# Three-piece hand-over of the first layer's one-hot tables, unread matmul streams in the second layer, zero-padded attribute matmul in the fourth

## The reference, cut to what matters

```python
h = jnp.maximum(_layernorm(x, axis=-1), 0.0)
x = x + _L0_gnn_ref(h, edge_attr_32, L0_gnn_eps, src, dst)      # relu(h[src] + edge_attr), summed over dst
h = jnp.maximum(_layernorm(x, axis=-1), 0.0)
x = x + _L1_gnn_ref(h, src, dst, edge_attr_3, edge_attr_10, edge_weight, L1_gnn_W1, L1_gnn_W2)
...
x = x + _L2_gnn_ref(h, src, dst)                                # degree-normalized sum
...
x = x + _L3_gnn_ref(h, src, dst, edge_attr_4, edge_attr_8, L3_gnn_fc_w1, L3_gnn_fc_w2)
```

```python
h = 2.0 ** 0.5 * jax.nn.relu(emb @ W1 / 10.0 ** 0.5)
w = (h @ W2 / 16.0 ** 0.5).reshape(E, 7, MUL, MOUT)
...
s_act = TANH_GAIN * jnp.tanh(s_out)
gates = TANH_GAIN * jnp.tanh(g_out)
edge_ftr = jnp.concatenate([s_act, (gates[:, :, None] * v_out).reshape(E, 24)], axis=1) * norm[:, None]
return jax.ops.segment_sum(edge_ftr, edge_dst, num_segments=N)
```

## Time and profile before

| | |
|---|---|
| timed runs | 23265.71, 23264.34, 23223.69 us, median 23264.34 |
| the profiled execution | 23142.48 us (span 23140.8) |
| busy share of the span | PE 64%, PEld 47%, DVE 54%, ACT 32%, POOL 43% |
| granted TensorE clock, mean | 0.715 of full speed |
| layer 0, about 395 to 6394 us | clock 0.60 in the middle, DMA share 0.63 |
| layer 1, about 6500 to 16130 us | clock 0.70 |
| layer 3, about 17190 to 23070 us | clock 0.83 |

### The profile page before, as it was taken

One profiled execution on the slowest core, in us unless ns is written; L12 is line 12 of the kernel. 1 busy time (PEld: TensorE's weight loads), 2 busy tenths in 40 slices (PEclk: granted clock), 3 DMA queues, 4 the chain that ended last, 5 costly groups with the idle time before them and its releaser, 6 DMA issues. The chain is left out here.

```text
span 23140.8 us, 410176 instructions
## 1 busy us (share of the span) xinstructions
PE 14747.1 (64%) x107469; PEld 10941.2 (47%) x108092; DVE 12537.1 (54%) x29165; ACT 7316.3 (32%) x22555; POOL 10030.6 (43%) x11407
## 2 busy tenths in 40 slices
PE   2444443433357777777777777777667777777777
PEld 1333333333345555555555555555445555555555
DVE  5455444554445555555555555555026666666666
ACT  1333333333323333333333333333002222222222
POOL 4455444454434444444444444443014555555554
PEclk7565655566667776777767777776888888888887
DMA  4666666666611111111111111110851111111111
GB/s 89 80 87 88 83 82 81 84 84 82 79 29 20 20 20 20 20 20 20 20 20 20 20 20 20 20 20 16 341 222 17 17 17 17 17 17 17 17 17 17
DMA packets 3048984, 1153.55 MB, mean 50 GB/s; under 512 B 2631873, under 2 KB 2993198, under 8 KB 3047249
## 3 DMA queue, kind: packets, MB, share of 16 engines
q1 hardware_dynamic: 2236554, 930.37, 19.8%
q0 software_dynamic: 312320, 178.52, 5.7%
q10 hardware_dynamic: 500000, 43.28, 2.3%
HBM read 767.02 MB, written 383.38 MB: 50 GB/s over the span
## 5 line engine op out<-in xcount | busy, mean ns | idle before, releaser
L1349 POOL DMA_INDIRECT w_rows<-table,w_idx x9375 | 8966.0, 956 | 6981.3 <-issue 2969.3
L1574 PE MATMUL w_p_w<-w_w,w_ht 128*128 128x256 f32 x12500 | 3743.4, 454 | 746.8 <-DVE w_prodv L1516 378.7
L1331 PE MATMUL w_p_deg<-w_hot_lo,w_hot_row 128*128 128x196 bf16 x6250 | 1956.2, 355 | 2574.5 <-issue 1210.7
L1574 PEld LDWEIGHTS w_p_w<-w_w,w_ht 128*128 128x128 f32 x12500 | 2762.7, 229 | 1717.7 <-issue 639.4
L1925 PE MATMUL w_p_xe<-w_xt,w_pick_b 128*128 128x128 bf16 x12500 | 1691.8, 279 | 1998.9 <-ACT w_xt L1911 1810.3
L1787 DVE TENSOR_TENSOR w_prod<-w_p_xe,w_he 128x512 f32<-128x512 f32 x3125 | 2123.7, 688 | 1012.7 <-PE w_p_xe L1925 999.1
L1734 POOL TENSOR_TENSOR w_dots<-w_v,w_unit 128x240 f32<-128x240 f32 x625 | 400.1, 640 | 4518.6 <-issue 3491.5
L1925 PEld LDWEIGHTS w_p_xe<-w_xt,w_pick_b 128*128 128x128 bf16 x12500 | 1032.9, 122 | 2762.5 <-ACT w_xt L1911 1665.2
L1145 ACT ACTIVATE w_dist<-row_iota,w_negrel 128x32 f32<-128x32 f32 x9375 | 2178.8, 313 | 442.6 <-issue 262.8
L1305 ACT CAST w_counts<-w_p_count 128x784 bf16<-128x784 f32 x1875 | 1237.1, 705 | 3410.6 <-remote 2107.1
L1331 PEld LDWEIGHTS w_p_deg<-w_hot_lo,w_hot_row 128*128 128x128 bf16 x6250 | 878.3, 141 | 2756.8 <-issue 1855.5
(11 more groups left out here) (209 smaller groups left out, 21512.5 us busy)
## 6 DMA issues: line engine op xcount, KB each, us to landing
counts<-w_counts SPq DMA_DIRECT2D x1250, 245.0 KB
d_rows<-counts SPq DMA_DIRECT2D x388, 784.0 KB
w_rows<-table,w_idx POOLq DMA_INDIRECT x9375
w_rel_row<-rel_row SPq DMA_DIRECT2D x625, 120.0 KB
w_edge<-e SPq DMA_DIRECT2D x625, 80.0 KB
w_idx<-src SPq DMA_DIRECT2D x1875, 2.5 KB
w_negrel<-negrel SPq DMA_DIRECT2D x1875, 2.5 KB
w_nodes<-split SPq DMA_DIRECT2D x1875, 2.0 KB
```

Source lines behind the costliest of these rows:

```text
L1331: nc.tensor.matmul(p_deg[:], hot_row[s2][:, b, :], hot_lo[s2][:, b, :], start=False, stop=False, skip_group_check=True)
L1349: pool.indirect_dma_start(out=rows[:, t, :], out_offset=None, in_=table[0:N, :], in_offset=bass.IndirectOffsetOnAxis(ap=idx[:, t:t + 1], a ...
L1574: last = nc.tensor.matmul(p_w[:, t * 256:(t + 1) * 256], ht[g.slot(2)][:, k, t * P:(t + 1) * P], w2[:, k, :], start=k == 0, stop=k == 1)
```

## The change

Three edits, one for each of the loops:

```diff
@@ window_pass_0, DVE
-                    vec.tensor_tensor(hot_row[s2][:], spread(p_iota[:, 0:P], [P, PAIRS_G, P], 1),
-                                      spread(pair[s][:, :, 0], [P, PAIRS_G, P], 2), ALU.is_equal)
+                    for b0, b1 in PIECES:
+                        bs, n = slice(2 * b0, 2 * b1), 2 * (b1 - b0)
+                        vec.tensor_tensor(hot_row[s2][:, bs, :], spread(p_iota[:, 0:P], [P, n, P], 1),
+                                          spread(pair[s][:, bs, 0], [P, n, P], 2), ALU.is_equal)
+                        vec.tensor_tensor(hot_lo[s2][:, bs, :], spread(p_iota[:, P:], [P, n, SRC_LO], 1),
+                                          spread(pair[s][:, bs, 1], [P, n, SRC_LO], 2), ALU.is_equal).then_inc(pair_hot_ready, 1)
                     done(dve, emb_high, g)
                     free(dve, emb_low, g, 1)
                     vec.tensor_sub(emb_rest[:], emb[s][:], emb_parts[s][:, 0, :]).then_inc(emb_left, 1)
-                    vec.tensor_tensor(hot_lo[s2][:], spread(p_iota[:, P:], [P, PAIRS_G, SRC_LO], 1),
-                                      spread(pair[s][:, :, 1], [P, PAIRS_G, SRC_LO], 2), ALU.is_equal).then_inc(pair_hot_ready, 1)
@@ window_pass_0, PE
-                    done(pe, pair_hot_ready, g)
                     for i, (b0, b1) in enumerate(PIECES):
+                        pe.wait_ge(pair_hot_ready, g.times(len(PIECES), i + 1))
                         wait_count(pe, count_moved, g.times(len(PIECES), i + 1 - len(PIECES)))
@@ window_pass_3: setup, then DVE, then PE
-        hidden = StackedEmbedding(nc, a, 3, sb, HID3)
+        hidden = StackedEmbedding(nc, a, 3, sb, HID3, P)
+        still = sb("still", [P, P + 256], BF16)
+            vec.memset(still[:], 0.0)
                         wait_count(pe, w_used, g.times(len(BANKS), bank + 1 - len(BANKS)))
+                        if t1 == T:
+                            for _ in range(4):
+                                nc.tensor.matmul(p_w[:, T * 256:], still[:, 0:P], still[:, P:], start=True, stop=True)
@@ window_pass_1, PE
+            def stream(times):
+
+                for _ in range(times):
+                    nc.tensor.matmul(p_he[:, 0:512], ident_b[:], pick_b[:].rearrange("p i e -> p (i e)"), start=True, stop=True)
+
                     wg.product(pe, g)
                     free(pe, he_ready, g, 1)
                     free(pe, xt_ready, g, 2)
+                    stream(6)
                     for c0, c1 in ((0, 512), (512, GE)):
```

## The result

The changed kernel takes 23972.81 us in the median of three runs (23908.48 to 24071.28), against 23264.34 before: a ratio of 1.0315 with a 95% interval of 1.0256 to 1.0374, +708 us. The forecast was 23812, slower, in 23050 to 24300.

The account below looks back on a forecast made before the run. It took a loop of waits, not a full engine, to bound layer 1. Terms of 745 - 200 + 0 gave +545 us on the profiled 23142; scaled to the timed median, 23812 us, range 23050 to 24300.

Parts of the forecast that it names:

- Layer 1, every round long: Layer 1: the streams make ACT's cast start behind POOL's gather burst in every group; 16.55 us a group, +745 us.
- The 0.3 us for the held expansion: Layer 1: the last expansion's signal may be held in the burst too; 0 to 0.6 us a group, taken as 0.3.
- a cast cannot be released inside the burst when its matmuls are not done in it: Layer 1: transposes delayed to around or past the burst's end make the cast late, costing 0.89 us a group.
- The clock: Layer 1: streams fill PE before the idle stretch, not in it, so `p_out` still takes 2.39 us.
- the first rival: Layer 1: streams keep the clock at full through `p_out`; 15.05 us a group, -195 us, whole kernel 22870; chance 13%.
- Layer 0, -200 us: Layer 0: PE starts earlier on pieces, saving two fifths of SP's wait; -200 us, in -480 to +150.
- Layer 3, 0 us: Layer 3: the four added matmuls hide in PE's idle time and zero rows add no columns; 0, between -100 and +200.
- PE's idle 2.07 us a group would take in the added work: Layer 3: PE's idle time hides four matmuls of 256 columns, +250 to +500 us if nothing hid them.
- The sum: Whole kernel: 745 - 200 + 0 = +545 us on the profiled execution of 23142 us, giving 23687.

Follow-up runs that it names:

- the first pair: The kernel before and the fully changed kernel as first measured: 23264.34 us and 23972.81 us, ratio 1.0315.
- `e5_all`: All three layers' edits together against the kernel before, on another chip with held signals: 23610.27 us against 22960.0, ratio 1.0292.
- the second run: Layer 1's six streams ahead of the transposes; alone, added to the kernel before: 23027.15 us against 22960.0, ratio 1.0041.
- The first run: Layer 1's six streams ahead of the hidden units; alone, added to the kernel before: 23721.85 us against 22960.0, ratio 1.0324.
- `e2_streams`: Only layer 1's twelve streams added to the kernel before, on a chip without held signals: 17390.86 us against 15797.12, ratio 1.1008.
- `e10_early_and_pieces`: Kernel before with layer 0's three pieces, layer 1's transposes ahead of the last expansion and ACT's cast ahead of its vector-weights copy: 22706.23 us, ratio 0.9801.
- `e13_narrow_stills_again`: Kernel before with only layer 3's four zero matmuls, 16 columns wide, no zero rows, signals held: 23349.3 us against 23158.21, ratio 1.008.

## Why the prediction was right in the time and wrong in two steps

- **Layer 1, every round long**: right. 45% of the rounds were long before and 100% after, at 16.51 us, with 16.55 forecast (+719 us against +745). The 0.3 us for the held expansion was +0.26 over 16.25 in the first pair, but `e5_all`, the same kernel, has just 16.25, so that term lies within the scatter.
- **Layer 1, what makes them long**: wrong. The step that failed is "a cast cannot be released inside the burst when its matmuls are not done in it", with the second run as its cause. It was never put to use: the transposes were to end at or past the burst's end, 3.7 us or more later, but with both runs they end 2.5 us later and still 1.4 us ahead of that end. Alone, the second run costs 0.4%; its transposes end 1.1 us later and the share of long rounds stays at 49%. The first run does it alone (+3.2%, 100% long), by carrying the last expansion and the vector weights deeper into the burst, ahead of the transposes' signal. I had priced that as a side effect of 0 to 0.6 us; it was the cause. That layer 1 came out within 26 us is therefore partly luck: with both runs in the kernel, either cause makes every round long, and a long round's length had been read from the trace of before.
- **The clock**: right for `p_out`. The mean in layer 1 rose from 0.70 to 0.78, but `p_out` took 2.40 us in the place where it took 2.39. By the groups by line (count, busy us, mean ns of one), here of the changed kernel from 7200 to 15400, then of `e2_streams`, where the clock was 1.00, a matmul of it took 420 ns and not 280:

```profile
L1981 PE MATMUL w_p_low<-w_stack,w_sgt 128*128 128x64 f32 x4969 | 1164.9, 420 | 13.3 <-ACT w_sgt L1868 7.3
```

```profile
L1974 PE MATMUL w_p_low<-w_stack,w_sgt 128*128 128x64 f32 x5390 | 715.4, 280 | 49.2 <-ACT w_sgt L1861 30.8
```

  The streams did move the clock, though. Counted from the trace's clock record, in the median group full clock came 0.3 us behind the burst's start and ended 0.7 us behind its end before; in the changed kernel it came 0.4 us ahead of the start and ended 2.5 us behind the end. `p_out` starts 3.6 to 3.8 us behind it, so 4% of its matmuls ran in under 350 ns, and 13% in `e5_all`, where full clock lasted until 3.1 us behind the end. That may be why layer 1 is shorter there than with the first run alone, 16.25 against 16.57; it was not tested. So the first rival had begun to come true, without reaching `p_out` in most groups. The rule of the Trainium skill, page "TensorE: Matmul & The Clock Gate", section "HAM oscillation — how this bites in real kernels", is not refuted: no run here put a stream into the pause. In the runs without held signals there is no such pause, the clock is 1.00, and there the streams only cost.
- **Layer 0, -200 us**: the right sign; the size lies in the scatter. The first pair has -50 us. In one comparison on a shared chip it is 9.12 us a group (`e5_all`) against 9.67, 9.60 and 9.47 in the three kernels with the old layer 0; in another, 5000/547 = 9.15 (`e10_early_and_pieces`) against 9.49. That is -210 to -340 us. In the first pair SP's wait fell by 364 us, from 417.6 to 53.3, and the layer gained only 50: the shrinking of that wait, by which I had sized the term, does not give the gain. Without held signals the pieces gain 312 us of 15797.
- **Layer 3, 0 us**: wrong, +300. The step that failed is that PE's idle 2.07 us a group would take in the added work. The work could be hidden; the four instructions could not, by `e13_narrow_stills_again`, since inside a burst PE at times gets on only one matmul in 1.4 us. The 0.75 us in the earlier trace rows, which I took for a wait for DVE, has "issue" in the row. On the chip without held signals the edit costs +2 us, as priced.
- **The sum**: +545 us for the profiled execution, where the two traces differ by 929. The layer 3 that was missing (300) and the smaller gain in layer 0 (150), less 26 in layer 1, make 424 us more than forecast, to be held against 384; the windows of the three layers add up to 969, 40 above the difference of the spans. The medians differ by 708, since the profiled executions are the slowest after and one below the median before. That the forecast misses the median by only 161 us is luck to that extent.

Left open: what holds the signals, and what makes one round long and the next short in the same kernel. The traces show that the holding goes with POOL's gathers and is on signals that PE gives: where the cast ran inside a burst, ACT's signal of it reached PE with 0.06 us (median of 284 groups before). It was there on two of the four chips of these runs and in the first pair. Each chip was seen in one batch of runs, so the chip itself and its state at the time are not told apart; no run here changed it. Whether PE's slow steps in layer 3 and the held signals are one thing was not tested, nor was a stream in the pause, nor were PE's and ACT's moves one by one.

## What to carry to other kernels

Filling an engine that is idle on average is free only if nothing behind the filling has a deadline: ask which signals it pushes past what comes next, and count instructions as well as their time. Before adding matmuls for the clock, find in the windows where the clock is low and whether the filling stands in that stretch. And when one wait is at the head of a loop, moving its signal forward in the order of sender and receiver gained 2.2% in layer 1 here for no added work, until a later signal became the wait.

## What the runs showed of the hardware

- The same kernel took 15797 to 15977 us on two chips and 22960 to 23264 on others, with the same durations of its gathers (0.94 us, 0.30 apart). By layer it is 7.50 against 9.57 us a group in layer 0, 8.38 against 15.36 in layer 1 and 6.67 against 9.38 in layer 3, with a granted clock of 1.00 against 0.70 and 0.83 in the last two. In layer 1 the traces show the late signals as the difference, with the pause and the lower clock that follow; how layers 0 and 3 divide was not worked out.
- Where signals are held, one that PE gives some 2 us or more into a burst of gathers is late: the transposes' signal, 2.2 us into it, was taken up 1.3 us behind the last gather's end in 45% of the groups before, and inside the burst but still over 1.5 us late in most others. Signals given within the first 1.5 us were taken up after 0.04 us (medians; expansion 0.9 us, vector weights 1.4 us into the burst).
- In the same bursts PE can be slowed to one matmul in about 1.4 us without a wait for a semaphore in the profile. Four added matmuls of 16 columns a group, 0.065 us of work each, cost 0.39 us a group in layer 3 (0.31 by the time of the whole kernel); without held signals they cost nothing.
- One stream of 512 bf16 columns takes 0.217 us at full clock.
